# Cross-attention with a routed feed-forward layer: where the filler stands in an attention step

## The reference

```python
q = einsum('oc,bct->bot', Wq, layernorm(x)) + bq
k = einsum('oc,bcs->bos', Wk, ctx) + bk
v = einsum('oc,bcs->bos', Wv, ctx) + bv
dot = mask * einsum('bhdt,bhds->bhts', q, k) / 4 - (1 - mask) * 1e6
x = x + einsum('bhts,bhds->bhdt', softmax(dot) * mask, v)
h = layernorm(x).reshape(2048, 512)
top2 of softmax(h @ gate_w.T), their weights normalized to sum 1
x = x + sum over the two experts e of weight_e * (silu(h @ w1g_e.T) * (h @ w1u_e.T)) @ w2_e.T
```

## Time and profile before

| | us |
|---|---|
| median of 3 runs | 956.54 (954.77 to 958.49) |
| the profiled execution | 951.4 |
| its span, first to last instruction | 949.6 |
| PE busy | 810.5 (85% of the span) |
| DVE busy | 538.6 (57%) |
| ACT busy | 316.7 (33%) |
| POOL busy | 377.2 (40%) |
| raw score pairs, PE L985 | 157.2 busy |
| scores, PE L972 | 154.6 busy |
| value products, PE L1001 | 137.2 busy |
| maxima, DVE L731 | 308.7 busy, 256 instructions |

### The profile page before, as it was taken

The page is one execution under the profiler, slowest core; times in us unless marked ns, Lnnn a source line. Parts: engine busy times, 40 slices in busy tenths (PEclk is TensorE's granted clock), DMA queues, the critical chain, the costliest instruction groups (busy, mean ns, idle before and its releaser), DMA issues. The chain is left out here.

```text
span 949.6 us, 12844 instructions
## 1 busy us (share of the span) xinstructions
PE 810.5 (85%) x3737; PEld 366.5 (39%) x3738; DVE 538.6 (57%) x1038; ACT 316.7 (33%) x615; POOL 377.2 (40%) x396
## 2 busy tenths in 40 slices
PE   2178999999998999999999983189999999999994
PEld 1022233333332333333333321155555555555552
DVE  2177888888887888887878722412323232322322
ACT  0003656555656555555556672000000000000000
POOL 5634445555755665566554324301111111111111
PEclk9677999999999999999999996589999999999998
DMA  4553467665866676657455322413635365363332
GB/s 120 169 177 113 145 206 222 187 221 177 268 195 193 210 224 197 201 181 210 134 177 156 125 92 90 143 46 67 147 58 155 57 156 146 66 146 62 59 66 34
DMA packets 84287, 137.69 MB, mean 145 GB/s; under 512 B 14600, under 2 KB 40520, under 8 KB 84240
## 3 DMA queue, kind: packets, MB, share of 16 engines
q1 hardware_dynamic: 68512, 107.97, 37.4%
q0 software_dynamic: 7744, 17.86, 9.6%
q10 hardware_dynamic: 7984, 11.28, 4.2%
HBM read 77.34 MB, written 59.36 MB: 144 GB/s over the span
## 5 line engine op out<-in xcount | busy, mean ns | idle before, releaser
L731 DVE TENSOR_REDUCE mx<-tile 128x2 f32<-128x1024 f32 x256 | 308.7, 1217 | 64.8 <-PE tile L985 61.3
L629 ACT ACTIVATE pr<-sc 128x512 f32<-128x512 f32 x512 | 268.8, 601 | 191.5 <-PE sc L972 189.0
L985 PE MATMUL tile<-qk 97*128 97x512 bf16 x512 | 157.2, 390 | 47.6 <-DVE mx L731 22.4
L1283 POOL DMA_INDIRECT out_dram<-y,ids x36 | 56.1, 1559 | 282.5 <-DVE ids L1208 278.4
L972 PE MATMUL sc<-qk 100*128 100x512 bf16 x512 | 154.6, 382 | 7.7 <-DMA qk<-mxt 5.1
L1001 PE MATMUL pvb<-pr,vp 128*32 128x512 f32 x1024 | 137.2, 608 | 0.0
L1263 ACT ACTIVATE sg<-gp 128x352 f32<-128x352 f32 x36 | 16.7, 465 | 291.3 <-PE up L1312 291.3
L1333 PE MATMUL dp<-wring,at 128*128 (+1 forms) x216 | 102.2, 609 | 13.4 <-DVE at L1218 13.4
L985 PEld LDWEIGHTS tile<-qk 97*128 97x128 bf16 x512 | 36.4, 98 | 185.7 <-DVE mx L731 83.0
L1312 PE MATMUL gp<-wring,xtile 128*128 x288 | 93.7, 469 | 2.1 <-DVE meta L1199 2.1
L554 POOL TENSOR_SCALAR parts<-qkf 128x512 bf16<-128x512 f32 x32 | 48.4, 1513 | 113.3 <-DVE qkf L812 112.4
(11 more groups left out here) (118 smaller groups left out, 723.9 us busy)
## 6 DMA issues: line engine op xcount, KB each, us to landing
qk<-stack_d SPq DMA_DIRECT2D x32, 768.0 KB
stack_d<-parts SPq DMA_DIRECT2D x32, 384.0 KB, 2.6
wring<-w_dram SPq DMA_DIRECT2D x32, 352.0 KB, 6.3
xl<-routed_d ACTq DMA_DIRECT2D x38, 257.0 KB, 2.7
stack_d<-parts SPq DMA_DIRECT2D x32, 256.0 KB, 2.9
pv_d<-ov SPq DMA_DIRECT2D x32, 256.0 KB, 4.1
xin<-x_dram SPq DMA_DIRECT2D x16, 256.0 KB, 5.7
cin<-ctxt_dram SPq DMA_DIRECT2D x8, 512.0 KB, 6.2
```

Source lines behind the costliest of these rows:

```text
L629: nc.scalar.activation(pr[s % 2][:, j, :], sc[(32 * u + 4 * s + j) % NSC][:, :], ACT.Exp, scale=SCALE).then_inc(exped.sem, 1)
L731: dve.tensor_reduce(mx[:, half(w), 2 * j:2 * j + 2], t[:, :, :], X, ALU.max, negate=True).then_inc(drained.sem, 1)
L985: last = nc.tensor.matmul(t[:, i, :], qs[half(w)][0:RAW_ROWS, h, c * P:c * P + P], ks[half(w)][0:RAW_ROWS, h, :], start=True, stop=True)
L1283: pool.indirect_dma_start(out, bass.IndirectOffsetOnAxis(ap=ids[:, k, :], axis=0), y[:, k, :], None, compute_op=ALU.add).then_inc(y_added, 16)
```

## The change

In each step PE's filler moves from the end of the step to the place between the second pair of scores and the value product. The second raw pair of the step is now its last piece. In step 7 the ranks stay behind the value product, and the k projection goes ahead of it. `tile_events` follows, since the two slots are given out in PE's order. DVE's readings are put in the same order: the addition of the bias to the values (L825) and to the projections (L812), the copy of the logits (L755) and the split of the maxima (L742 to L748) now stand ahead of the maximum of the step's second raw pair. ACT's copy of the transposed tokens (L610) moves from behind the first exponential of step 5 to behind the last one of step 4.

```diff
@@ tile_events
-        if s == 7:
-            ev += max_[:1] + ["ranks"] * has(n - 2) + max_[1:] + ["k"] * has(n + 3)
-            continue
-        ev += max_
+        ev += max_[:1]
...
+        if s == 7:
+            ev += ["k"] * has(n + 3) + ["ranks"] * has(n - 2)
+        ev += max_[1:]
@@ scalar, unit
-                        if (s, j) == (5, 0) and has(u - 2):
-                            transposed_out(u)
+                    if s == 4 and has(u - 2):
+                        transposed_out(u)
@@ vector, unit
+                values_out(u)
                 maximum(u, 7)
                 token_stats(u, 1)
-                values_out(u)
...
+                projection_out(u, 0)
                 maximum(u, 11)
...
-                projection_out(u, 0)
...
                 normalize(u)
+                choose(u, 0)
                 maximum(u, 15)
-                choose(u, 0)
                 choose(u, 1)
...
                 choose(u, 4)
+                split_maxima(u)
                 maximum(u, 1)
                 choose(u, 5)
-                split_maxima(u)
 
                 maximum(u, 2)
+                projection_out(u, 1)
                 rows_of(u, 0)
                 maximum(u, 3)
                 rows_of(u, 1)
-                projection_out(u, 1)
@@ tensor, unit
-                    if s == 0 and has(u - 1):
-                        product(u - 1, 7)
-                    if s and has(u):
-                        product(u, s - 1)
-                    if s == 7:
-                        ranks(u)
-                    for m in todo[1:]:
-                        raw_scores(u, m)
                     if s == 1:
                         values(u)
...
                     if s == 7:
                         project(u, 1)
+                    if s == 0 and has(u - 1):
+                        product(u - 1, 7)
+                    if s and has(u):
+                        product(u, s - 1)
+                    if s == 7:
+                        ranks(u)
+                    for m in todo[1:]:
+                        raw_scores(u, m)
```

## The result

The changed kernel takes 978.82 us (977.94 to 979.27, 4 runs) against 955.65 of the kernel before on the same chip: a ratio of 1.025 with a 95% interval of 1.022 to 1.028. It is 23 us slower. I had forecast 5.8 us slower, with 970 as the upper end of the range. The sign was right and the size was not. The two profiled executions, 951.4 and 977.9, lie 26.5 apart, since the one of the kernel before was faster than its median.

What follows compares the result with a forecast made beforehand. PE was taken to set the attention stage's pace, with DVE close behind. 7.7 - 2.5 - 0.4 + 1 = +5.8 us on the profiled 951.4 gave 957.2, and 962 for the median of runs; range 950 to 970.

Steps and rivals of the forecast that it cites:

- The holes: PE's waits behind tokens, logits and transposed maxima in the old order, 0.60, 0.37 and 0.93 us, 1.90 per unit.
- The wait of 0.18 ahead of each filler: A filler needs the last step's second slot: 1.74 us of PE work against 1.92 until release, so at least 0.18.
- The entry to the value product: Extra time before a value product that follows a filler, kept at 0.09 us, with bounds of nothing and 0.20.
- rival 3: Much slower: entering the value product behind a float32 filler costs 0.20 us, six a unit; +7 us, 969; chance 0.12.
- DVE's chain of 6.06 + c: DVE's work from raw pair 15 to the k projection's slot; PE has 4.7 us there, so stands 1.36 + c.
- c: Time of DVE's cast of the indices in that chain: 0.26 us when free, 0.81 when held, 0.7 as mean.
- held instructions of the split: Two instructions of DVE's split of the maxima might be held by POOL's operations: +1 us, bounds 0 and +3.
- The hole ahead of the q projection is about the same in both orders.: PE's wait ahead of the q projection was taken as about unchanged, adding nothing to the sum.
- Units without all the token work: Two units without token work trade a hole of 0.93 us for four waits of 0.18: -0.4 us.
- The transfer: Scores' waits for the transfer of the split maxima, 5.1 us, would about halve: -2.5 us, bounds 0 and -5.1.
- The sign: Slower by over 0.5% had chance 0.48, within 0.5% 0.38, faster 0.14; the sum was +5.8 us.
- Rival 1: Faster: DVE keeps up, holes go and five fillers lose only 0.18 us each; 943 us; chance 0.16 with its neighbour.

Runs made afterwards that it cites:

- e10: The kernel before with only one filler, the values, in the new place; 969.5 us, ratio 1.014 to the kernel before.
- e13: The kernel before with transposed tokens and transposed maxima in the new place, batch normalization behind pair 12, whole split ahead of pair 1's maximum; 942.59 us (0.986).
- e2: The changed kernel with DVE's two token normalizations each one maximum later, behind pairs 9 and 10; 969.16 us, ratio 1.015 to the kernel before.

## Why the prediction was right in sign and wrong in size

- **The holes.** Right. Waits for a maximum at raw pairs fell by 9 us, and those for the logits went. In the full units 1.90 a unit was there to lose.
- **The wait of 0.18 ahead of each filler.** Mis-sized. The slot's release was right, but the weights of a filler that waits for its slot are loaded only behind the wait, and my sum had no term for that. Ahead of tokens and logits the wait is 0.27. Ahead of the values it is 0.25 here and 0.18 in e10; here DVE runs three maxima in a row behind L799 and is 0.1 late for the slot; that the hold of L799 does this was not tried. Together the longer waits are 0.24 a unit.
- **The entry to the value product.** The 0.09 was right, and rival 3 was wrong. The distance from filler to product less the filler's old length is 0.09 behind the transposed maxima and the q projection, 0.11 behind the tokens, 0.15 behind the logits, 0.18 and 0.19 behind the k projection and the values. But what is above 0.09 is in the fillers and not in the product: from before to after the rows of the fillers grew by 0.10 (values, 1.95 to 2.05), 0.08 (k, 1.90 to 1.98), 0.07 (logits, 0.96 to 1.03) and 0.02 (tokens), and those of the q projection and the transposed maxima did not. It is the other part of the late weights: 0.27 a unit, 3 us over 11 units. In e13 the tokens don't wait, and the product starts 0.53 behind them, their 0.44 and 0.09.
- **DVE's chain of 6.06 + c.** Right in size, partly by luck. I had 2.06 for all waits from pair 15 to the k projection; in the unit shown they are 0.27 + 0.40 + 1.26 = 1.93, which is also the mean of the ten full units. I had split them otherwise, about 1 ahead of raw pair 1 and 0.8 ahead of the k projection. The cast lasted 0.49 on the mean, so c was 0.58 and not 0.7: in seven units it was free (0.17) and the third instruction of the split was held instead (0.81 to 0.85), in three it was held (1.20 to 1.29), the split was free, and raw pair 1 came 1.4 to 1.5 late. For held instructions of the split I had 1 us in all.
- **"The hole ahead of the q projection is about the same in both orders."** This is the step that failed, the largest single term of the miss: 6 us over the ten full units. The hole went from 0.24 to 0.82, 0.6 a unit, since the values' move sets the token normalization and POOL's multiply on the same release. I had looked for the lock only where the long chain was. e2 and e10 show it: with the normalization later the hole is 0.18, and the values alone bring it. The next in size are the waits and the late weights of the two points above, together 0.51 a unit, 5 us.
- **Units without all the token work.** Wrong. I had -0.4, and the first three lost 4.6. In them raw pair 0 waited for its stack of q and k (1.50 and 0.70 us at 140.38 and 174.47), and the k projection up to 1.86. Why the stack lands later was not tried.
- **The transfer.** About right: 2.1 us less instead of 2.5.
- **The sign.** Slower had a chance of 0.48 with me. Its margin of 5.8 us was made of a chain that was sized right; most of the other 17 us came from terms that my sum had at nothing.

Per full unit: 0.70 as forecast, 0.59 at the q projection, 0.27 of longer fillers and 0.24 of longer waits ahead of values, tokens and logits, less 0.13 in the chain and 0.14 behind the ranks, gives 1.53; measured are 1.52 for the ten units (15.2 us). Rival 1 was right in a half that my sum did not use: the holes are worth having for the two shortest fillers, with DVE's order fitted to POOL's. Values and logits cost time in the new place; the two projections were never moved alone.

## What to carry to other kernels

With two slots by turns, a short piece of work (0.11 and 0.44 us here) gained where other work stands between it and the next user of the slot; a long one (0.81 and 1.79) hides the read-out itself and cost time there. Whatever waits for a slot also loses the loading of its weights ahead of time, up to 0.1 us here. A change of order on one engine shifts two others against each other: write down, for every instruction of DVE between SBUF operands near the chain, which instruction of POOL it will lie beside, at all places and not only at the one that looks critical. The place to look first is where one instruction releases both.

## What the runs showed that I had not expected

- A held normalization lasts less than the wait and its own length together: begun 0.09 and 0.11 behind POOL's 1.04 and 1.15 us it took 1.24 and 1.33, where the rest of POOL's and its free 0.54 would make 1.49 and 1.58. In the changed kernel POOL's L559, an instruction with one input, held none: the batch normalization stayed 0.54 inside L559's 1.6 us in all nine units of the stretch. That one input is the reason is not shown: in the kernel before, at 41.85 us, it took 0.94 with an instruction of one input (L554) begun 0.05 behind it.
- A value product on 32 columns costs 0.09 us to enter, behind bfloat16 scores and behind every filler alike, once the fillers' own longer rows are taken off.
